# A layer of adaptive norm, TTT and mixture of experts on 8 cores: another order of the prologue, and of the routed rows at the end

## The reference, cut to what matters

```python
mod = (silu(c) @ wmod).reshape(4, 6, 1, -1)          # sa, ca, ga, sb, cb, gb
h = layernorm(x) * (1 + ca) + sa
x = x + ga * ttt(h, theta_K, theta_V, theta_Q, W0, b0)   # per token: one SGD step on W, then W @ q + b
h = layernorm(x) * (1 + cb) + sb
shared = silu(h @ shared_gate_w) * (h @ shared_up_w) @ shared_down_w
routed = sum over the 2 best of 8 experts: score * (silu(h @ gate_w[e]) * (h @ up_w[e])) @ down_w[e]
x = x + gb * (shared + routed)
```

## Time and profile before

| | us |
|---|---|
| median of 3 runs | 1592.87 |
| lowest and highest run | 1587.56, 1785.51 |
| the profiled execution | 1584.75 |
| its span, on core 7 (slowest) | 1583.2 |
| TensorE busy on core 7 | 1407.4 (89%) |
| VectorE, ScalarE, GpSimd busy | 734.0, 493.7, 300.9 |
| span of the fastest core (2) | 1542.5 |

### The profile page before, as it was taken

One profiled execution on the slowest core, in us unless ns is written; L12 is line 12 of the kernel. 1 busy time (PEld: TensorE's weight loads), 2 busy tenths in 40 slices (PEclk: granted clock), 3 DMA queues, 4 the chain that ended last, 5 costly groups with the idle time before them and its releaser, 6 DMA issues.

```text
span 1583.2 us, 22747 instructions; the slowest of 8 cores (1542.5 to 1583.2 us)
## 1 busy us (share of the span) xinstructions
PE 1407.4 (89%) x7825; PEld 700.6 (44%) x7825; DVE 734.0 (46%) x1278; ACT 493.7 (31%) x784; POOL 300.9 (19%) x209
## 2 busy tenths in 40 slices
PE   0488889898999898999998899999989799999897
PEld 0343444444454454544543444644434344444353
DVE  2526565757463655656546524532222222223676
ACT  1145444444455444435434321122112111111010
POOL 0038876813400001001001110000000000001130
PEclk9999999999999999999998999999999999999998
DMA  9964356525774522122174477489999999976663
GB/s 237 254 129 134 107 149 132 173 67 113 205 148 120 110 74 85 63 85 81 45 169 148 106 203 169 130 202 191 205 209 200 218 167 204 194 141 228 225 213 133
DMA packets 82373, 244.16 MB, mean 154 GB/s; under 512 B 7365, under 2 KB 7493, under 8 KB 77638
## 3 DMA queue, kind: packets, MB, share of 16 engines
q0 software_dynamic: 47440, 112.75, 36.1%
q1 hardware_dynamic: 26870, 92.05, 17.6%
q10 hardware_dynamic: 7936, 37.75, 9.6%
HBM read 262.46 MB, written 78.64 MB: 215 GB/s over the span
## 4 chain that ended last, share of the span: by engine, by line
PE 67%; DMA 16%; DVE 9%; issue 5%; POOL 1%; ACT 1%; SPq 0%; DVEq 0%; POOLq 0%; ACTq 0%
PE prep L668 9%; PE u L932 7%; DMA w0u<-uw 6%; PE u L830 5%; PE gate L901 5%; PE up L901 4%; PE up L898 4%; PE gate L898 4%; PE up L733 4%; PE up L760 3%; PE prep L932 3%; PE gate L733 3%; DMA ygb<-yx,sl 3%; DMA w1u<-suw 3%; DMA wmb<-wmod 3%
## 5 line engine op out<-in xcount | busy, mean ns | idle before, releaser
L1420 DVE TENSOR_TENSOR act<-up,sgb 128x512 bf16<-128x512 f32 (+1 forms) x128 | 84.1, 658 | 312.6 <-PE up L901 194.0
L1088 ACT ACTIVATE sgb<-gate 128x512 bf16<-128x512 f32 (+1 forms) x128 | 73.0, 570 | 460.3 <-PE gate L901 226.4
L1296 DVE TENSOR_TENSOR WT<-WT,u 128x512 f32<-128x512 f32 x240 | 153.2, 680 | 43.4 <-PE u L830 43.1
L830 PE MATMUL u<-Gsb,Ktk 128*128 128x512 bf16 x480 | 125.8, 385 | 29.8 <-DVE WT L1296 28.7
L668 PE MATMUL prep<-hft,s_thK 128*128 128x512 bf16 x512 | 122.1, 386 | 7.8 <-ACT hft L997 3.4
L1058 ACT CAST Wbf<-WT 128x1024 bf16<-128x1024 f32 x120 | 124.7, 1041 | 6.8 <-DVE WT L1296 6.7
L1607 POOL DMA_INDIRECT hx<-h2m,sl x28 | 29.1, 1039 | 430.5 <-DVE sl L1403 424.8
L1549 POOL TENSOR_SCALAR x2b<-x2b,silc 128x1024 f32<-128x1024 f32 x28 | 79.9, 2852 | 19.9 <-DMA x2b<-wmod 19.0
L830 PEld LDWEIGHTS u<-Gsb,Ktk 128*128 128x128 bf16 x480 | 43.2, 98 | 86.1 <-issue 49.3
L668 PEld LDWEIGHTS prep<-hft,s_thK 128*128 128x128 bf16 x512 | 50.0, 99 | 70.7 <-issue 16.2
L1029 ACT ACTIVATE Kft<-prep,kb 128x512 bf16<-128x512 f32 x64 | 44.0, 687 | 113.6 <-PE prep L668 113.6
(11 more groups left out here) (250 smaller groups left out, 2303.9 us busy)
## 6 DMA issues: line engine op xcount, KB each, us to landing
hx<-zero ACTq DMA_DIRECT2D x4, 5120.0 KB, 31.3
x2b<-wmod POOLq DMA_DIRECT2D x32, 512.0 KB, 5.4
yx<-ring SPq DMA_DIRECT2D x32, 512.0 KB, 6.8
xb<-x SPq DMA_DIRECT2D x19, 512.0 KB
wmb<-wmod SPq DMA_DIRECT2D x8, 1024.0 KB, 13.6
x2b<-x SPq DMA_DIRECT2D x16, 512.0 KB, 4.5
hx<-zero ACTq DMA_DIRECT2D x4, 2048.0 KB, 11.9
pair<-gw POOLq DMA_DIRECT2D x4, 2048.0 KB, 30.1
```

The source lines that it names most:

```text
L830: m = t.matmul(U[jh][:, 0:512], Ktk[s % 2][:, cc * D + dt * P:cc * D + (dt + 1) * P], Gsb[:, cc * D + jh * 512:cc * D + (jh + 1) * 512], s ...
L1296: v.tensor_add(w, w, U[jh][:, 0:512]).then_inc(S["v_W"], 1)
L1420: v.tensor_mul(act[k % 2][:, fj * ACW:fj * ACW + COLS[k]], R[2 + n % 2][:, 0:COLS[k]], sgb[n % 2][:, 0:COLS[k]]).then_inc(v_act, 1)
```

## The change

The modulation sums are split: `mc` adds the eight tiles of ca, one output row of 0.5 MB each, and `ms` after it those of sa. Six such loads are in flight (MODS) in place of three of 1 MB. `colc` makes the columns of ca alone and scales theta_K, which is now loaded into another buffer (`thKr`, the space of `Wbf`) and scaled into `thK`. Five `k` groups of block 0 follow; then `ms`, then `cols` for sa and the bias (from the unscaled `thKr`), then the last three `k` groups. Block 0's groups go to six banks `K0` that the scan doesn't use yet, so that only groups 6 and 7 wait for an eviction. GpSimd issues theta_K's load ahead of its memsets; ScalarE issues the loads of the first four x chunks and of the constants, which SyncE did. GpSimd asks for theta_V when 11 of the 16 sums are done. Some semaphores are joined.

At the end, block 0 of the second half no longer waits for routed rows: `finish_block` adds its halves to z, and `add_routed` comes after it, in the column phase of the block after the next; chunks 0 to 3 are stored when their routed rows are in. The places are steps 0 to 7 of the full blocks and steps 0, 2, 4, 6 of the last; on odd cores two chunks are left over (`Z_LATE`), added after the last column phase and ahead of the last block's finish. `NY` is 6 on odd cores: the gathers use `ygb` and `zx`, three chunks; on even cores it stays 4, two chunks.

```diff
@@ -26,6 +26,7 @@
+MODS = 6
@@ -72,9 +73,12 @@
-out += [("ln", 0), ("xn", 0), ("x", 0), ("mod", 0), ("ln", 1), ("xn", 1), ("x", 1), ("mod", 1),
-        ("ln", 2), ("xn", 2), ("x", 2), ("mod", 2), ("ln", 3), ("xn", 3), ("x", 3), ("mod", 3), ("cols",)]
-out += [("k", 0, et) for et in range(DT)]
+for g in range(4):
+    out += [("ln", g), ("xn", g), ("x", g), ("mc", g)]
+out += [("mc", dt) for dt in range(4, DT)] + [("colc",)]
+out += [("k", 0, et) for et in range(5)] + [("ms", dt) for dt in range(DT)] + [("cols",)]
+out += [("k", 0, et) for et in range(5, DT)]
@@ -244,10 +248,14 @@
+if step[:2] == ("k", 0):
+    continue
...
+elif kind == "colc":
+    uses = [[("v_col", 1)]]
 elif kind == "cols":
-    uses = [[("v_col", 1)], [("v_kc", 1)]]
+    uses = [[("v_col", 2)], [("v_kc", 1)]]
@@ -370,6 +378,8 @@
+K0 = R + U
@@ -396,8 +406,10 @@
+thKr = Wbf
 with ExitStack() as mctx:
-    wmb = mctx.enter_context(nc.sbuf_tensor("wmb", [P, 3 * 2 * D], F32))
+    wmb = mctx.enter_context(nc.sbuf_tensor("wmb", [P, MODS * D], F32))
@@ -537,8 +549,20 @@
-Z_AFTER = dict(zip([(S1 + 1, fj) for fj in range(4, 8)]
-                   + [(S1 + 2 + i, fj) for i in range(NGR - 2) for fj in range(1, 7)], range(NCH)))
+Z_PLACES = [(S1 + 2 + i, fj) for i in range(NGR - 2) for fj in (range(DT) if i < NGR - 3 else range(0, DT, 2))]
+Z_AFTER = dict(zip(Z_PLACES, range(NCH)))
+Z_LATE = range(len(Z_PLACES), NCH)
+NY = 4 if NCH > 16 else 6
+def y_place(c16, k2):
+    n = 2 * c16 + k2
+    i = n % NY
+    t, o = (ygb, i * D) if i < 4 else (zx, (i - 4) * D)
+    return ld_yg[i], n // NY + 1, t[:, o:o + D]
@@ -579,9 +603,11 @@
-    if pair:
-        return ((ga_bc, cb_bc), (sb_bc, cb_bc))[pair - 1]
-    return sb_bc, cb_bc
+    return ((ga_bc, cb_bc), (sb_bc, cb_bc))[pair - 1]
+def first_block_bank(et):
+    return K0[et % 6]
@@ -608,24 +634,29 @@
+elif kind == "colc":
+    b = A[BANK[step, 0]]
+    t.wait_ge(v_mod, DT)
+    free_bank(t, step)
+    for i in range(DT):
+        m = t.matmul(b[:, i:i + 1], cb_bc[:, i * P:(i + 1) * P], ones_f[:, 0:1],
+                     start=True, stop=True)
+    m.then_inc(S["p_col"], 1)
...
-    for i in range(2 * DT):
-        a_ = mod_sums(0)[i // DT]
-        m = t.matmul(b[:, i:i + 1], a_[:, (i % DT) * P:(i % DT + 1) * P], ones_f[:, 0:1],
+    for i in range(DT):
+        m = t.matmul(b[:, i:i + 1], sb_bc[:, i * P:(i + 1) * P], ones_f[:, 0:1],
...
-    t.wait_ge(ld_thK, 16)
-    t.wait_ge(S["v_col"], 1)
+    after(t, "v_col", *step)
...
-    for dt in range(DT):
-        for et in range(DT):
-            m = t.matmul(b2[:, et:et + 1], thK[:, dt * D + et * P:dt * D + (et + 1) * P],
-                         sa_b[:, dt:dt + 1], start=(dt == 0 and et == 0),
-                         stop=(dt == DT - 1 and et == DT - 1))
-        m.then_inc(S["p_kc"], 1)
+    for et in range(DT):
+        for dt in range(DT):
+            m = t.matmul(b2[:, et:et + 1], thKr[:, dt * D + et * P:dt * D + (et + 1) * P],
+                         sa_b[:, dt:dt + 1], start=(dt == 0), stop=(dt == DT - 1))
+    m.then_inc(S["p_kc"], 1)
@@ -658,11 +689,17 @@
-b, w = A[BANK[step, 0]], thK if kind == "k" else thQ
+w = thK if kind == "k" else thQ
...
-free_bank(t, step)
+if kind == "k" and j == 0:
+    b = first_block_bank(et)
+    if et >= 6:
+        after(t, "a_k", "k", 0, et - 6)
+else:
+    b = A[BANK[step, 0]]
+    free_bank(t, step)
@@ -1026,7 +1063,8 @@
-s_.activation(dst[:, o:o + n], A[BANK[step, 0]][:, 0:n], AF.Identity,
+b = first_block_bank(et) if kind == "k" and j == 0 else A[BANK[step, 0]]
+s_.activation(dst[:, o:o + n], b[:, 0:n], AF.Identity,
@@ -1159,21 +1197,29 @@
-elif kind == "mod" or kind == "row":
-    pair, tiles = (0, (2 * arg[0], 2 * arg[0] + 1)) if kind == "mod" else (1 + arg[0], arg[1:])
+elif kind == "mc" or kind == "ms":
+    dt, a_ = arg[0], cb_bc if kind == "mc" else sb_bc
+    n = dt if kind == "mc" else DT + dt
+    if n == 0:
+        v.wait_ge(a_c, 1)
+    v.wait_ge(ld_wm[n % MODS], 16 * (n // MODS + 1))
+    w = wmb[:, (n % MODS) * D:(n % MODS + 1) * D]
+    if dt == 0:
+        v.tensor_scalar_mul(a_[:, :], w, silc[:, 0:1]).then_inc(v_mod, 1)
+    else:
+        v.wait_ge(v_mod, n)
+        v.scalar_tensor_tensor(a_[:, :], w, silc[:, dt:dt + 1], a_[:, :],
+                               op0=ALU.mult, op1=ALU.add).then_inc(v_mod, 1)
+elif kind == "row":
+    pair, tiles = 1 + arg[0], arg[1:]
...
-        if n == 0:
-            v.wait_ge(a_c, 1)
...
-        if pair:
-            v.wait_ge(ld_row[n % 2], 16 * ((n - DT) // 2 + 1))
-            stage, o = row_stage(n - DT)
-        else:
-            v.wait_ge(ld_wm[dt % 3], 16 * (dt // 3 + 1))
-            stage, o = wmb, (dt % 3) * 2 * D
+        v.wait_ge(ld_row[n % 2], 16 * ((n - DT) // 2 + 1))
+        stage, o = row_stage(n - DT)
@@ -1183,19 +1229,23 @@
+elif kind == "colc":
+    b = A[BANK[step, 0]]
+    after(v, "p_col", *step)
+    own_.then(v.tensor_scalar_add(cac[:, 0:DT], b[:, 0:DT], 1.0))
+    v.tensor_scalar(cac[:, DT:2 * DT], b[:, 0:DT], -1.0, -1.0, op0=ALU.mult,
+                    op1=ALU.add).then_inc(S["v_col"], 1)
+    v.wait_ge(ld_thK, 16)
+    own_.wait()
+    for dt in range(DT):
+        m = v.tensor_scalar_mul(thK[:, dt * D:(dt + 1) * D], thKr[:, dt * D:(dt + 1) * D],
+                                cac[:, dt:dt + 1])
+    m.then_inc(S["v_thK"], 1)
...
-    v.wait_ge(S["p_col"], 1)
-    v.tensor_copy(sa_b[:, :], b[:, 0:DT])
-    v.tensor_scalar_add(cac[:, 0:DT], b[:, DT:2 * DT], 1.0)
-    v.tensor_scalar(cac[:, DT:2 * DT], b[:, DT:2 * DT], -1.0, -1.0, op0=ALU.mult,
-                    op1=ALU.add).then_inc(S["v_col"], 1)
-    v.wait_ge(S["v_col"], 1)
-    for dt in range(DT):
-        v.wait_ge(S["p_kc"], dt + 1)
-        m = v.tensor_scalar_mul(thK[:, dt * D:(dt + 1) * D], thK[:, dt * D:(dt + 1) * D],
-                                cac[:, dt:dt + 1])
-    m.then_inc(S["v_thK"], 1)
+    after(v, "p_col", *step)
+    v.tensor_copy(sa_b[:, :], b[:, 0:DT]).then_inc(S["v_col"], 1)
+    v.wait_ge(S["p_kc"], 1)
@@ -1452,22 +1502,26 @@
-        if hh == 0:
+        if hh == 0 and j:
...
+        elif hh == 0:
+            v.wait_ge(ld_z[0], 16)
...
-    if hh:
+    if hh and i and j == 0:
+        own_.then(m)
+    elif hh:
...
 for k2 in range(2):
-    v.wait_ge(ld_yg[c16 % 2][k2], 16 * (c16 // 2 + 1))
-    if k2:
+    landed, n, rows = y_place(c16, k2)
+    v.wait_ge(landed, 16 * n)
+    if k2 or c16 < 4:
...
-    q = ((c16 % 2) * 2 + k2) * D
-    m = v.scalar_tensor_tensor(z[:, o:o + D], ygb[:, q:q + D],
+    m = v.scalar_tensor_tensor(z[:, o:o + D], rows,
@@ -1506,6 +1560,9 @@
+if k == NB:
+    for c16 in Z_LATE:
+        add_routed(c16)
@@ -1513,19 +1570,19 @@
 def gpsimd_prog(g, own_, flag_reg):
-    g.wait_ge(v_mod, 2 * DT - 6)
+    g.wait_ge(v_mod, DT + 3)
...
-    w_cast(g, thQ, d_thQ, ld_thQ)
-    g.dma_start(rw_bf[:, :], ap(d_rw, 0, [[NE, P], [P * NE, DT], [1, NE]])).then_inc(ld_rw, 16)
+    w_cast(g, thQ, d_thQ, ld_Qrw)
+    g.dma_start(rw_bf[:, :], ap(d_rw, 0, [[NE, P], [P * NE, DT], [1, NE]])).then_inc(ld_Qrw, 16)
...
-        g.wait_ge(S["p_col"], 1)
+        g.wait_ge(S["p_col"], 2)
@@ -1635,13 +1692,13 @@
 for k2 in range(2):
-    if c16 >= 2:
-        g.wait_ge(v_z, c16 - 1)
-    q = ((c16 % 2) * 2 + k2) * D
+    if c16 >= NY // 2:
+        g.wait_ge(v_z, c16 - NY // 2 + 1)
+    landed, _, place = y_place(c16, k2)
...
-        ygb[:, q:q + D], None, ap(d_yx, 0, [[D, rows], [1, D]]),
+        place, None, ap(d_yx, 0, [[D, rows], [1, D]]),
...
-    ).then_inc(ld_yg[c16 % 2][k2], 16)
+    ).then_inc(landed, 16)
@@ -1674,10 +1731,10 @@
-elif kind == "mod":
-    for dt in (2 * arg[0] + 3, 2 * arg[0] + 4):
-        if dt < DT:
-            load_mod(sy, dt)
+elif kind == "mc":
+    load_mod(sy, arg[0] + MODS)
+elif kind == "ms" and DT + arg[0] + MODS < 2 * DT:
+    load_mod(sy, DT + arg[0] + MODS)
@@ -1788,7 +1845,11 @@
-sy.wait_ge(v_out, c16 + 1)
+if c16 < 4:
+    sy.wait_ge(v_z, c16 + 1)
+else:
+    sy.wait_ge(v_out, c16 - 3)
@@ -1820,10 +1881,17 @@
-s_.wait_ge(ld_b0, 16)
+s_.dma_start(s_ident[:, :], d_ident[:, :]).then_inc(ld_const, 16)
+s_.dma_start(xb[:, :], x_rows(0)).then_inc(ld_x[0], 16)
+s_.dma_start(b_f32[:, :], d_b0[:, :]).then_inc(ld_cb0, 16)
+for g in range(1, 4):
+    t_, o = x_place(g)
+    s_.dma_start(t_[:, o:o + D], x_rows(g)).then_inc(ld_xp[g - 1], 16)
+for dst, src in ((mtri, d_mtri), (s_mut1, d_mut1), (s_ebase, d_ebase), (s_slot, d_slot)):
+    s_.dma_start(dst[:, :], src[:, :]).then_inc(ld_const, 16)
+s_.wait_ge(ld_cb0, 32)
...
-s_.wait_ge(ld_c, 16)
@@ -1837,40 +1905,35 @@
+    w_cast(g, thKr, d_thK, ld_thK)
...
-    w_cast(g, thK, d_thK, ld_thK)
...
-def load_mod(sy, dt):
-    if dt >= 3:
-        sy.wait_ge(v_mod, 2 * (dt - 2))
-    o = (dt % 3) * 2 * D
-    sy.dma_start(wmb[:, o:o + 2 * D],
-                 ap(d_wmod, dt * P * 6 * D, [[6 * D, P], [1, 2 * D]])).then_inc(ld_wm[dt % 3], 16)
+def load_mod(sy, n):
+    if n >= MODS:
+        sy.wait_ge(v_mod, n - MODS + 1)
+    row = 1 if n < DT else 0
```

(16 more changed lines are left out.)

16 lines of the change are left out of this document (8 added, 8 removed).

## The result

| | before | changed |
|---|---|---|
| median | 1589.45 us, 21 runs | 1569.35 us, 21 runs |
| lowest | 1582.43 | 1562.01 |
| profiled execution | 1584.75 | 1565.17 |
| ratio, 95% interval | | 0.9859 (0.9841 to 0.9877) |

The change is worth 1.4%, by the ratio 22.4 us (0.0141 x 1589). That is under the 2% line, and 10 us less than the 32.4 predicted. The time of 1569 lies inside the range given, 13 above the forecast of 1556.

A forecast was written before the change was run, and what follows sets the result against it. Core 7, an odd core, was taken to bound the kernel, through chains of waits at its front and tail. Prologue 18.4 plus tail 14 made 32.4 us, from 1588.4 to 1556; range 1546 to 1573.

The forecast's parts named there:

- The path is then the last `sb` sum. I take it at 56.0: Prologue: K's last groups wait for the final modulation sum, put at 56.0 us against 59.4 before.
- rival E: Prologue: banks don't overlap, all eight K groups run after the bias; prologue gain 9, time 1565, chance 0.05.
- The half pace: Prologue: first K group behind the bias's one-column matmuls runs at half pace, 3.45 us; full rate would save 1.7.
- Not released by a transfer: Sign in the profile after: ScalarE's W0 cast comes near 81.5 us without waiting for W0 to land.
- 14 predicted: Tail, odd cores: 16.4 us gained, less 2.5 for waits on gathers; bounds 7 and 17.
- About 15: Prologue, even cores: gain of about 15 us, less than on odd cores because of theta_Q.
- Joining semaphores: nothing: Prologue: joined semaphores cost nothing, being below the other waits.
- Net about 5 gained: Tail, even cores: first block's stall goes, slower chunk pairs and slow restarts cost some; about 5 us gained.
- The floor that I put 25 us lower: Whole kernel before: even cores end some 25 us below core 7, the odd core that sets the time.
- rival C: Even cores become the bound: prologue gains 6, tail nothing, core 0 ends 1.8 after core 7; 1558, chance 0.07.
- Rival A: Tail: three gathers in flight collide with stores, banks fill again; tail gain 6, time 1564, chance 0.20.
- Rival B: Prologue: theta_K lands late, at 47, with three queues sharing; five groups end at 61, time 1561, chance 0.10.

The follow-up runs named there:

- th_late: Changed kernel with theta_K asked for after the fourth ca sum (some 32 us) instead of at 1.6; ran once, 1573.95 us.
- p_warm: Changed kernel with 15 unused wide matmuls before the ca columns and 16 behind them; ran once, 1559.35 us.
- t_two: Changed kernel with two chunks of gathered rows in flight on odd cores too, instead of three; ran once, 1581.56 us.
- t_bufs: Changed kernel with two more chunks of gathered rows in flight on every core; median 1583.79 us against 1598.46 for the kernel before.
- t_both: Changed kernel with two more gathered chunks in flight, and chunks 4 and 5 taken first; 1561.8 us, ratio 0.9823 to the kernel before.
- p_rw: Changed kernel with the router's weights on their own semaphore, so Q's columns wait for theta_Q alone; ratio 0.9854 to the kernel before.
- p_x45: Changed kernel with the loads of x chunks 4 and 5 put behind the last ca tile's sum; ran once, 1570.75 us.

## Why the prediction was off

**The prologue on odd cores: 18.4 predicted, 13.5 to 13.9 measured.** The step that failed is "The path is then the last `sb` sum. I take it at 56.0". It ended at 62.45. The number stood on the transfers alone (one sum instead of two, the hole gone), and not on VectorE's order, which puts eight sums (0.75 + 9.61) behind theta_K's scaling, and that (3.26) behind the ca columns (3.54) and the last ca sum. For 56.0 the last ca sum had to end at 38; it ended at 44.6. The text did weigh theta_K's landing, and allowed it till 41.5; it landed at 43.4, but even then the columns, at 48.4, were later. The ca tiles themselves were never costed. th_late shows what they paid: 7 us for theta_K, with which the full engines write 220 to 290 GB/s. The 354 GB/s I took for the rate come from the window after theta_K had landed. Of the 6.5 us, 1.7 came back, since the sa columns ran behind K groups and took 1.84 instead of the 3.5 predicted, and some 0.3 in hand-overs: 70.1 + 6.5 - 2.0 = 74.6, as measured. (The last addition of the prediction's chain is 0.2 too high: 69.2 and 0.7 are 69.9; the hand-overs here take that in.) So the sign and the mechanism were right (five groups beside the sa tiles, in banks of their own: rival E is out) and the size was a third too large.

**The half pace.** The group behind the bias took 3.41 us, as the row of before said it would, with the granted clock of 65 to 70 us at 0.67, partly the lower level; it is 0.53 from 67.0 to 70.3 alone. Kept at work on wide matmuls (p_warm), TensorE ran the columns and the first K groups at full pace. By the Trainium skill (TensorE: Matmul & The Clock Gate, "What's actually happening") activity releases the clock, and p_warm agrees by the lengths, 1.84 us against 3.54, while the granted clock reads 1.00 in both. For the one-column matmuls of the bias the row was the better guide: in p_warm, too, the group behind them took 3.57, at a granted clock of 0.50. In the first K group of the changed kernel the granted clock reads 1.00 while 16 matmuls take 5.62 us and the next 16 take 3.62, so there the length of a matmul is the safer sign.

**W0.** "Not released by a transfer", near 81.5: it came at 86.68, released by W0's landing (0.66 us). theta_V, "near the same time" in the prediction, is asked for by the eleventh sum, and that sum was late with the others: 56.1 on core 1, where the kernel before asked at 50.7.

**The end on odd cores: 14 predicted, 13.8 measured.** Its steps hold: no stall in the first down-projection, 13.8 us for it, three chunks nearly hide a gather. Its split doesn't: 9.1 of it stood for the finish that no longer waits, but with two chunks in flight that finish alone leaves 1.9 (t_two), and 11.9 of the 13.8 hang on the third chunk. The late chunks were cheap (2.3 us of TensorE's time in t_bufs), and not the 7 that I expected of t_both.

**Even cores: 20 predicted, 2.7 measured in the mean of the profiled pair.** Over the runs they even end later: 1551.0 in the mean, 1546.6 before (19 runs). Two steps failed. "About 15" for their prologue: theta_Q "is asked for no earlier and now meets its use" was written down and then not subtracted, and it landed 8.0 us later than before, not at the same time. It took 12.8 of the 14.2 us. "Joining semaphores: nothing" holds for odd cores alone; on even ones it is 2.5 to 3.2 of these (p_rw). "Net about 5 gained" for their end: it is 1.7 lost. With eight chunks in a row and two in flight, what was one stall of 11.5 us on core 0, with two short ones of 3.7 together, became three, of 3.5, 4.7 and 6.8, each with a group at half pace behind it; t_bufs, with four in flight, has none.

**The slowest of eight.** The floor that I put 25 us lower came up to the odd cores. Over the changed kernel's runs the odd cores' mean span is 1557.6 and the even ones' 1551.0; in 5 of 16 runs an even core was the slowest, in the kernel before in none of 19. The slowest odd core averages 1564.5, the slowest of all 1565.2, so this costs 0.7 us of time. That is rival C, by its cause and under its price of 1.8.

**The sum.** 13.5 + 13.8 = 27.3 on odd cores. Over the runs the slowest odd core's span fell from 1588.8 (19 runs of before in three comparisons) to 1564.5, by 24.3, and with the even cores 23.6; the ratio gives 22.4 with an interval of 2.9 either way. Of the 10 us between forecast and result, the prologue is 4.9, the end 0.2, the even cores 0.7; 3 to 4 can't be placed. I had set myself a limit of 5 us for a change in the length of the middle stage. The profiled pair breaks it: from the first V group to the second shared half the odd cores took 7.3 us longer, core 7 5.3. The odd cores' mean span over the runs fell by 24.6 (1582.2 to 1557.6), which leaves 2.7 for the middle, and one trace of each kernel doesn't tell 7.3 from that, with cores that scatter by 5 to 9. The sum put this stage at nothing. Core 1 waited 21.8 us for experts' weights where it had waited 13.4, but core 7 waited 13.7 where it had waited 17.1. No one cause shows in all four odd cores. The remaining 3 of the 13 between 1556 and 1569 are no gain lost: the kernel before measured 1589.45 and not 1588.4, and a median stands against a ratio.

Rival A is out (gather waits of 3.3 and 3.6 us). Rival B was right that theta_K is slower with three queues (9 us later), wrong in what it delays: the ca tiles, not the five groups alone.

## What to carry to other kernels

Where a transfer's landing is moved forward, write down the landing of every transfer that shares the engines with it, with a converting load counted by the bytes that it reads, and then walk the waiting engine's own order from there; a rate read in one window doesn't hold for the next. In a program whose time is the slowest of eight cores, give the changed cost of every role the same care: a gain on one role is worth no more than the distance to the next, and in the mean less. Latency of gathers is bought off with buffers: ask for what space has just come free before moving work around.

## What the runs showed of the hardware

- With a load that converts fp32 to bf16 among the transfers, the full engines write 220 to 290 GB/s; 329 without it at the same place (th_late), 354 after it. Per MB that it reads it holds the engines no longer than a plain load (4.6% against 5.1% of 66 us, th_late).
- Taking 1 MB of later loads away from behind a tile on the same queue moved it by under 0.5 us (p_x45); theta_K on another queue cost the ca tiles 7 us (th_late).
- Sixteen fp32 matmuls with one output column took 3.54 us behind an idle stretch and 1.84 behind wide matmuls, with the granted clock at 1.00 in both (changed kernel, p_warm).
- An even core's end fell by 21 us for two more chunks in flight and not a byte less moved (t_bufs).
